# A convolution of 17 taps evaluated at seven points: first quadruple of taps padded by two, 33 tap products in place of 34

## What is computed

```python
xc = jnp.transpose(x, (0, 2, 1))
h = _bn(_conv1d(xc, conv1_w, 0), ...)
h = jax.nn.relu(h)
h = _bn(_conv1d(h, conv2_w, 8), ...) 
x_conv = jnp.transpose(jax.nn.relu(h + xc), (0, 2, 1))
```

## Time and profile before

| what | value |
|---|---|
| median of 3 runs | 396.8 us |
| profiled execution: its time, and its span | 396.49 us, 394.7 us |
| PE busy | 366.2 us (93% of the span), 2191 matmuls |
| DVE, ACT, POOL busy | 320.8, 228.7, 221.3 us |
| mean granted clock of PE | 0.99 |
| one group, from the first taps of one to those of the next | 44.7 us |
| prologue until the first taps of group 1 | 42.0 us |

### The profile page before, as it was taken

The page is one execution under the profiler, slowest core; times in us unless marked ns, Lnnn a source line. Parts: engine busy times, 40 slices in busy tenths (PEclk is TensorE's granted clock), DMA queues, the critical chain, the costliest instruction groups (busy, mean ns, idle before and its releaser), DMA issues.

```text
span 394.7 us, 6487 instructions
## 1 busy us (share of the span) xinstructions
PE 366.2 (93%) x2191; PEld 319.6 (81%) x2191; DVE 320.8 (81%) x669; ACT 228.7 (58%) x423; POOL 221.3 (56%) x195
## 2 busy tenths in 40 slices
PE   2969795999999999999999999999999999999974
PEld 2847784988888998988888998989888898988954
DVE  4899879698688976998788976998778976987564
ACT  4535464463776467664676458563675548472773
POOL 3659262287437763486537763495537773395343
PEclk9999899899999999999999999999999999999999
DMA  7500000430101200120101301130101301000011
GB/s 240 207 0 1 2 2 0 159 109 1 55 21 36 105 23 33 55 106 2 53 0 53 106 0 53 53 106 0 53 2 53 108 2 55 1 2 0 2 53 53
DMA packets 7991, 19.39 MB, mean 49 GB/s; under 512 B 672, under 2 KB 5024, under 8 KB 6944
## 3 DMA queue, kind: packets, MB, share of 16 engines
q1 hardware_dynamic: 7536, 18.50, 13.6%
q10 hardware_dynamic: 432, 0.59, 0.4%
HBM read 14.90 MB, written 4.19 MB: 48 GB/s over the span
## 4 chain that ended last, share of the span: by engine, by line
PE 67%; DVE 22%; issue 5%; ACT 3%; DMA 1%; POOL 1%; DVEq 0%; SPq 0%; ACTq 0%; POOLq 0%
PE conv L1217 24%; PE back L1217 23%; PE back L1315 7%; DVE xl L820 5%; DVE stats L988 3%; DVE usum L954 3%; PE front L1287 2%; DVE tail L1022 2%; PE conv L1265 2%; PE front L1315 2%; PE back L1366 2%; DVE sv L839 1%; PE front L1307 1%; DMA xv<-in_x_dram 1%; ACT nmph L615 1%
## 5 line engine op out<-in xcount | busy, mean ns | idle before, releaser
L1217 PE MATMUL conv<-sth,wh 128*128 128x256 f32 x238 | 74.5, 313 | 8.2 <-DVE wl L1041 4.6
L1217 PE MATMUL conv<-sth,wl 128*128 128x256 f32 x238 | 69.2, 291 | 0.0
L1217 PE MATMUL conv<-stl,wh 128*128 128x256 f32 x238 | 69.2, 291 | 0.0
L1217 PEld LDWEIGHTS conv<-sth,wh 128*128 128x128 f32 x238 | 46.5, 195 | 15.1 <-DVE wl L1041 4.8
L516 POOL TENSOR_TENSOR rstd<-rstd,minus_half 128x4 f32<-128x4 f32 (+1 forms) x34 | 36.1, 1063 | 35.6 <-DVE rstd L992 35.6
L534 POOL TENSOR_TENSOR amat<-amat,adjT 128x512 f32<-128x512 f32 x32 | 49.4, 1575 | 1.4 <-ACT amat L657 1.4
L521 POOL TENSOR_TENSOR xw<-xw,xv 128x512 f32<-128x512 f32 (+1 forms) x17 | 20.9, 1230 | 52.0 <-ACT xw L681 52.0
L1217 PEld LDWEIGHTS conv<-stl,wh 128*128 128x128 f32 x238 | 46.6, 196 | 0.2
L1217 PEld LDWEIGHTS conv<-sth,wl 128*128 128x128 f32 x238 | 46.3, 195 | 0.0
L615 ACT ACTIVATE sth<-sv 128x272 fp32r<-128x272 f32 (+1 forms) x35 | 18.1, 518 | 41.7 <-DVE sv L839 27.1
L528 POOL TENSOR_TENSOR tail<-xn,later_w 128x512 f32<-128x512 f32 (+1 forms) x17 | 29.8, 1756 | 4.3 <-DMA out_dram<-tail 2.6
(11 more groups left out here) (219 smaller groups left out, 1012.1 us busy)
## 6 DMA issues: line engine op xcount, KB each, us to landing
adjT<-in_adj_dram SPq DMA_DIRECT2D x8, 1024.0 KB, 4.9
out_dram<-tail SPq DMA_DIRECT2D x15, 256.0 KB, 2.2
xv<-in_x_dram SPq DMA_DIRECT2D x7, 512.0 KB, 3.3
gbuf<-in_gates_dram SPq DMA_DIRECT2D x1, 576.0 KB, 6.4
tail<-in_conv_dram ACTq DMA_DIRECT2D x2, 256.0 KB, 3.8
xv<-in_x_dram SPq DMA_DIRECT2D x2, 256.0 KB, 4.7
later_w<-in_later_dram SPq DMA_DIRECT2D x1, 452.0 KB, 6.3
tail<-in_conv_dram SPq DMA_DIRECT2D x1, 320.0 KB, 5.4
```

The costliest lines, as they stand in the source:

```text
L1217: ins = pe.matmul(bank, a, b, start=first and k == 0, stop=last and k == len(todo) - 1)
```

## The change

Three zero slots are put around the 17 taps, two ahead (`LEAD`) and one behind, so that there are five full quadruples: (0, 0, t0, t1), (t2, ...), ... (t14, t15, t16, 0). `coef[j]` is the row of slots j, j + 4, ... ZERO's row (j = 0) begins with a zero slot, and INF's row (j = 3) ends with one, so both need four products; the rows at the other points have five. 33 products in all. In the split groups ZERO's three matmuls of one tap go away, 21 in seven groups, and one fp32 product (two passes) in group 0.

The other edits follow from the padding. All combined rows have five slots, so every tap sum on DVE and POOL is of 128x640 elements, and ACT's two copies of the last tap are gone. POOL zeroes the three slots, and the sums wait for that (`ends_zeroed`). The data shift by two nodes against the taps: `h1_out` writes q = 0 and q = 1 of the product into places that are no longer at one distance, with one instruction for each, so two instructions of 256 columns for one of 512.

```diff
-NTAP = (5, 5, 5, 5, 5, 5, 4)
+LEAD, PLACES = 2, 5
+NTAP = (5, 4, 5, 5, 5, 5, 4)
...
-        c2raw = tail[:, 0:TAPS * P].rearrange("p (k o) -> p k o", k=TAPS)
+        padded = tail[:, 0:4 * PLACES * P].rearrange("p (k o) -> p k o", o=P)
+        c2raw = padded[:, LEAD:LEAD + TAPS, :]
+        coef = [padded[:, j:4 * PLACES:4, :] for j in range(4)]
...
-        traw = (gtaps[:, 10:15, :], c2raw[:, 0:TAPS:4, :], gtaps[:, 5:10, :], ataps[:, 5:10, :],
-                gtaps[:, 0:5, :], ataps[:, 0:5, :], c2raw[:, 3:TAPS:4, :])
+        traw = (gtaps[:, 10:15, :], coef[0][:, 1:5, :], gtaps[:, 5:10, :], ataps[:, 5:10, :],
+                gtaps[:, 0:5, :], ataps[:, 0:5, :], coef[3][:, 0:4, :])
...
                 pool.memset(minus_half[:, :], -0.5).then_inc(exponent_set, 1)
+                pool.memset(padded[:, 0:LEAD, :], 0.0).then_inc(ends_zeroed, 1)
+                pool.memset(padded[:, LEAD + TAPS:, :], 0.0).then_inc(ends_zeroed, 1)
...
                 streams2(0)
+                pool.wait_ge(ends_zeroed, 2)
                 pool.wait_ge(conv2_loaded, 64)
-                pool.tensor_tensor(ataps[:, 10:14, :], c2raw[:, 0:16:4, :], c2raw[:, 2:16:4, :],
-                                   ALU.add).then_inc(tap_sums_one, 1)
...
+                pool.tensor_tensor(ataps[:, 10:15, :], coef[0], coef[2], ALU.add).then_inc(tap_sums_one, 1)
+                pool.tensor_tensor(ataps[:, 0:5, :], coef[1], coef[3], ALU.add).then_inc(tap_sums_one, 1)
...
-                done(act.activation(h1[:, 2 * h:2 * h + 2, :, :, PAD:PAD + TQ].rearrange("p b r q m -> p (b r) q m"),
-                                    conv1_bank(h, ahead)[:, :].rearrange("p (c m q) -> p c q m", c=GB, q=2), ACT.Relu,
-                                    bias=bn[:, 2:3], scale=bn[:, 0:1]), H1_READY)
+                src = conv1_bank(h, ahead)[:, :].rearrange("p (c m q) -> p c q m", c=GB, q=2)
+                for q in range(2):
+                    rows_q = h1[:, 2 * h:2 * h + 2, :, 1 - q, PAD + q:PAD + q + TQ].rearrange("p b r m -> p (b r) m")
+                    last = act.activation(rows_q, src[:, :, q, :], ACT.Relu, bias=bn[:, 2:3], scale=bn[:, 0:1])
+                done(last, H1_READY)
...
-                last_tap = c2raw[:, TAPS - 1:TAPS, :]
-                act.activation(gtaps[:, 4:15:5, :], last_tap.to_broadcast([P, 3, P]), ACT.Copy).then_inc(tap_copies, 1)
-                act.activation(ataps[:, 4:10:5, :], last_tap.to_broadcast([P, 2, P]), ACT.Copy).then_inc(tap_copies, 1)
...
+                dve.wait_ge(ends_zeroed, 2)
                 dve.wait_ge(conv2_loaded, 64)
-                w0, w1, w2, w3 = (c2raw[:, k:16:4, :] for k in range(4))
+                w0, w1, w2, w3 = coef
...
-                taps_step(ataps[:, 5:9, :], w3, 4.0, w1)
-                taps_step(gtaps[:, 5:9, :], ataps[:, 5:9, :], 2.0, utaps[:, 0:4, :])
+                taps_step(ataps[:, 5:10, :], w3, 4.0, w1)
+                taps_step(gtaps[:, 5:10, :], ataps[:, 5:10, :], 2.0, utaps[:, 0:5, :])
...
+                at = 1 if n == ZERO else 0
...
                 for k in range(k0, k1):
-                    ins = products(conv_out(n), [weights(n, k) + (sth[:, n, :, k:k + TQ], stl[:, n, :, k:k + TQ])],
+                    ins = products(conv_out(n), [weights(n, k) + (sth[:, n, :, at + k:at + k + TQ],
+                                                               stl[:, n, :, at + k:at + k + TQ])],
```

More of the change, by code:

```diff
@@ L314, in gnn_kernel @@
         tap_sums_one = sem("tap_sums_one")
-        tap_copies = sem("tap_copies")
+        ends_zeroed = sem("ends_zeroed")
         def wait(eng, name, g, j):
@@ L557, in prologue @@
                 streams2(0)
+                pool.wait_ge(ends_zeroed, 2)
                 pool.wait_ge(conv2_loaded, 64)
-                pool.tensor_tensor(ataps[:, 10:14, :], c2raw[:, 0:16:4, :], c2raw[:, 2:16:4, :],
-                                   ALU.add).then_inc(tap_sums_one, 1)
-                pool.tensor_tensor(ataps[:, 0:4, :], c2raw[:, 1:16:4, :], c2raw[:, 3:16:4, :],
-                                   ALU.add).then_inc(tap_sums_one, 1)
+                pool.tensor_tensor(ataps[:, 10:15, :], coef[0], coef[2], ALU.add).then_inc(tap_sums_one, 1)
+                pool.tensor_tensor(ataps[:, 0:5, :], coef[1], coef[3], ALU.add).then_inc(tap_sums_one, 1)
                 pool.wait_ge(tap_sums_one, 2)
-                pool.tensor_tensor(gtaps[:, 0:4, :], ataps[:, 10:14, :], ataps[:, 0:4, :], ALU.add).then_inc(tap_sums_one, 1)
+                pool.tensor_tensor(gtaps[:, 0:5, :], ataps[:, 10:15, :], ataps[:, 0:5, :], ALU.add).then_inc(tap_sums_one, 1)
                 pool.wait_ge(tap_sums_one, 3)
-                pool.tensor_tensor(ataps[:, 0:4, :], ataps[:, 10:14, :], ataps[:, 0:4, :],
+                pool.tensor_tensor(ataps[:, 0:5, :], ataps[:, 10:15, :], ataps[:, 0:5, :],
                                    ALU.subtract).then_inc(tap_sums_one, 1)
@@ L728, in prologue @@
                 h1_out(0, 1)
-                act.wait_ge(tap_copies, 2)
                 act.wait_ge(tap_sums, 3)
@@ L1083, in taps_step @@
                     dve.scalar_tensor_tensor(out, a, scale, b, ALU.mult, ALU.add).then_inc(tap_sums, 1)
-                dve.scalar_tensor_tensor(gtaps[:, 10:14, :], w3, 0.5, w2, ALU.mult, ALU.add).then_inc(tap_sums, 1)
+                dve.scalar_tensor_tensor(gtaps[:, 10:15, :], w3, 0.5, w2, ALU.mult, ALU.add).then_inc(tap_sums, 1)
                 steps[0] += 1
-                taps_step(gtaps[:, 10:14, :], gtaps[:, 10:14, :], 0.5, w1)
-                taps_step(gtaps[:, 10:14, :], gtaps[:, 10:14, :], 0.5, w0)
+                taps_step(gtaps[:, 10:15, :], gtaps[:, 10:15, :], 0.5, w1)
+                taps_step(gtaps[:, 10:15, :], gtaps[:, 10:15, :], 0.5, w0)
                 first_diffs()
@@ L1092, in prologue @@
                 parts2(0)
-                taps_step(utaps[:, 0:4, :], w2, 4.0, w0)
-                taps_step(ataps[:, 5:9, :], w3, 4.0, w1)
-                taps_step(gtaps[:, 5:9, :], ataps[:, 5:9, :], 2.0, utaps[:, 0:4, :])
+                taps_step(utaps[:, 0:5, :], w2, 4.0, w0)
+                taps_step(ataps[:, 5:10, :], w3, 4.0, w1)
+                taps_step(gtaps[:, 5:10, :], ataps[:, 5:10, :], 2.0, utaps[:, 0:5, :])
                 dve.wait_ge(later_loaded, 16)
@@ L1100, in prologue @@
                 factors(0)
-                taps_step(ataps[:, 5:9, :], ataps[:, 5:9, :], -2.0, utaps[:, 0:4, :])
+                taps_step(ataps[:, 5:10, :], ataps[:, 5:10, :], -2.0, utaps[:, 0:5, :])
                 parts1(0)
@@ L1247, in first_taps @@
                     wait(pe, E_READY_H, 0, 1)
-                    pe.wait_ge(tap_copies, 2)
                     pe.wait_ge(tap_sums, 3)
@@ L1264, in first_taps @@
                 for k in range(NTAP[n]):
-                    ins = pe.matmul(conv_out(n), traw[n][:, k, :], sv[:, ROW[n], :, k:k + TQ], start=k == 0,
+                    at = k + 1 if n == ZERO else k
+                    ins = pe.matmul(conv_out(n), traw[n][:, k, :], sv[:, ROW[n], :, at:at + TQ], start=k == 0,
                                     stop=k == NTAP[n] - 1)
```

## The result

The changed kernel takes **402.85 us**, the median of six executions (402.70 to 403.58), against 397.22 us for the kernel before on the same chip, also six (396.58 to 398.42). The ratio is 1.0136, 95% interval 1.0119 to 1.0154: slower by 1.4%. The forecast was 400.6 us, with a range up to 402.4. The direction was right; the time lies 0.45 us above the range. The profiled execution took 403.04 us, its span is 401.2 us, 6.5 more than before.

A forecast was written before the change was run, and what follows sets the result against it. The prediction took the bound to be a chain through ACT's h1, POOL's token difference and a held DVE, not PE's matmuls. 2.7 + 1.45 - 0.36 = +3.8 us on 396.8 gave 400.6 us, range 398.0 to 402.4.

The forecast's parts named there:

- Part 2, the split: h1 in four instructions delays POOL's difference and held DVE: +0.45 us at each of six boundaries, 2.7; +0.22 in group 0.
- Part 3, the sums: Five slots instead of four in each tap sum lengthen POOL's row in the prologue: MINUS2's taps at 25.0, +1.45 us.
- Part 1, ZERO's tap: Three matmuls fewer in each of seven later groups: nothing in groups 2 to 7, -0.36 us once in group 1.
- that wait isn't the end: In group 1, DVE waits 1.86 us for PE's last gate product, which comes 0.36 us sooner, so DVE gains too.
- The clock: Rival: PE idles longer ahead of MINUS2 in the prologue; a second low-clock stretch would give 402.3 us; chance 0.10.
- The sum: Whole kernel: 2.7 + 1.45 - 0.36 = +3.8 us on the median of 396.8, 1.0% slower.
- PE is the bound: Rival: h1 and the sums stay under cover, 7 x 0.36 = 2.5 us gained, 394.3 us; chance 0.08.
- DVE isn't held: Rival: L992's 0.62 us are its own, only POOL's late end counts, 0.2 us a boundary; +2.3, 399.1 us; chance 0.11.
- The split costs less: Rival: four h1 instructions on ACT take 1.5 us, +0.1 a boundary; +1.7 in all, 398.5 us; chance 0.14.

The follow-up runs named there:

- the filled kernels: Idle PE products ahead of three waits: kernel before 394.39 us, split alone 397.75, sums alone 395.98, sums and four ZERO taps 396.49, whole change 399.48.
- experiment 4: The changed kernel with five taps at ZERO again, one of them over the zero slot: 403.59 us, ratio 1.0161.
- experiment 1: The changed kernel with h1 written by one instruction again, its two phase rows exchanged in memory: 399.62 us, ratio 1.0049.
- experiment 8: The changed kernel with DVE's two variances of the second norm moved behind both halves' statistics: 402.68 us, ratio 1.0111.
- experiment 2: The kernel before with h1 in two instructions of 256 columns for each half, at the old places: 400.83 us, ratio 1.0081.
- `after_filled`: The changed kernel with idle PE products ahead of three waits, one in group 0 and two in group 1: 399.48 us, ratio 1.0052.

## Why the prediction was right or wrong

- **Part 2, the split (2.7 in the boundaries, 0.22 in group 0): right in its mechanism, somewhat short in size.** Four instructions were to take 1.88 us and take 1.92; the held variance was to end with POOL's difference and does; DVE passes on 0.45 us in each period, as forecast. Kept from the lower clock, the split costs 3.4 by the medians where 2.9 stood. In that pair of profiles 3.0 of it comes in the six periods, 0.5 each. The 0.67 at the start isn't the split's alone: the first convolution itself starts at 7.43 us in one and at 6.78 in the other. The estimate of the Trainium skill (VectorE: DVE Perf Modes, the errata-adjusted cycle table) would have given 1.7 for the boundaries; 0.49 us more for two split instructions, in place of the estimated 0.29, decides against it. For the hold the rule of the Trainium skill (SBUF — State Buffer, "Who interferes with whom") stands: the trace agrees, at 0.62 and 1.10 us for an instruction of 0.17.
- **Part 3, the sums: right in its mechanism, short in size.** The +1.45 holds 0.22 of the split's, so 1.23 is the sums' own. They cost 1.6 in the filled kernels, and MINUS2's taps start at 25.48 where 25.0 was forecast. The other sums grew by 0.27, the term's figure, but the first from 1.72 to 2.13 us, and POOL's two stream sums ahead of them by 0.13 each. Those two, 0.14 and 0.26, the term had at nothing; with them it comes to 1.63.
- **Part 1, ZERO's tap: right for six boundaries, wrong for group 1.** Of the 0.36 us that the sum took off there, experiment 4 shows 0.23 and the filled kernels none: the pair differs by 0.5 the other way in the median and 0.2 in the span, and group 1 takes 49.96 us against 49.92. Part 1's step "that wait isn't the end", with its -0.36, fell, at least in part. Which wait takes the gain in group 1 I haven't shown.
- **The clock: a term taken for a rival.** This is the step with the largest single part. "A second low stretch would give 402.3" had a chance of 0.10, and the sum was made as if the clock stayed. The row of the stretch at 42 to 46 us showed one stretch; that at 69.7 to 73.1 I didn't look for, although PE is idle for 4.59 us ahead of it and for 2.64 ahead of the other. And the profiled execution, at a mean of 0.990, was one of those that lost least. In the profiles after, PE has 6.8 us more at 1.2 GHz, and the price of 1.7 us for a low stretch was right (4.11 - 2.44). In the medians the clock's part is smaller (0.5 to 0.9), since the other executions of the kernel before lose more than the profiled one.
- **The sum.** It said 3.8. At a full clock it is 4.7 (spans) to 5.1 (medians): 0.1 to 0.5 more for the split, 0.4 for the sums and up to 0.36 for ZERO's tap. With 0.5 to 0.9 for the clock it is the measured 5.6. The kernel before also stood 0.4 higher in this comparison than in the three runs shown (397.22 for 396.8). No single term was far off; all erred to the same side, and the range, which ended at the rival with the second low stretch, had no room for several together.
- **The rivals.** "PE is the bound" fell with experiment 4 and with the unchanged period in experiment 1. "DVE isn't held" fell with experiment 8. "The split costs less" fell with 1.92 us.

What stays open: why MINUS2's passes ran at the lower clock behind the same 3.20 us of idle time in experiment 2 and not before; and why `after_filled` spends 2.4 us outside its span (399.48 against 397.0 in the profiled execution) where the kernel before spends 1.8.

## What to carry to other kernels

One instruction split in two, 0.24 us dearer, cost 3 us here, because two engines behind it pass it on and the last is held without showing a wait: look for instructions of one form with two durations, and compare their ends with what the neighbour engine is doing. Make the clock a term of the sum: list every stretch at the lower level in the profile and the idle time ahead of it, ask what the change does to that idle time, and see from the clocks of the runs whether the profiled execution is a lucky one, leaving out what is low behind the last matmul. Where PE waits some microseconds and its next work is on the path, products that nobody reads can be worth more than the change: 3.4 us here.

## What the runs showed of the hardware

- **The lower clock isn't tied to the idle time alone.** It came behind 2.45 and 4.57 us in the changed kernel and behind 2.64 us in the earlier trace rows; behind 3.20 us it came in one profile and not in another. The Trainium skill (TensorE: Matmul & The Clock Gate, Part 1) says of a kernel's start that the number of slow matmuls varies from run to run, since the monitor isn't in step with the program. No run here counts slow matmuls over several executions; the spread of the kernel before, 396.2 to 399.3 us at mean clocks of 0.991 to 0.982, is in line with it.
- **The granted clock in the profile doesn't show the start.** In 0 to 23.5 us it reads 1.00 before the change, yet the first convolution's matmuls of 512 columns follow each other at 0.43 us; behind ten idle products they do so at 0.23.
- **A small DVE instruction can carry a large hold**: 128x4 elements, 0.17 us free, 1.10 us beside POOL's difference.
- **ACT pays for a second instruction**: four of 128x256 take 1.92 us, two of 128x512 1.43, though 561 ns against 768 for one suggests more (4 x 0.56 = 2.24, 2 x 0.77 = 1.54); the overlap of instructions in a row is part of the price.
